# Gates and ups of three pairs of chunks by seven block products, in a fused two-layer kernel on one core

## The chip, the cores and the metric

The kernel runs on 1 core of one Trainium2 chip. The metric is the device time of one execution in microseconds; three executions are shown for the kernel before. The engines are PE (TensorE), ACT (ScalarE), DVE (VectorE), POOL (GpSimd) and SP, which here only issues transfers.

## The reference

The input x is 2 x 1024 = 2048 tokens of 512 numbers. Two layers follow each other, each ending in a layer norm:

```python
x = layernorm(x + taylor(x) + (silu(x @ gate.T) * (x @ up.T)) @ down.T)   # gate, up: 1248 x 512
# layer 2: 56 blocks of 32 rows each; a low-rank score (16) picks one row in each block
inter = x @ c1.T @ c2.T                                  # 2048 x 1792
idx = argmax of each block of 32 in inter
h = relu(w1[idx] . x);  x = layernorm(x + sum over blocks of h * w2[idx])   # w1, w2: 1792 x 512
```

`taylor` is a sum of seven terms on 128 channels, done before the part that is changed. Layer 2 is computed densely: all 1792 products with w1, masked to the picked row of each block, then the product with w2.

## The kernel before

**Tiling.** The tokens form 4 groups (g) of 512, each of 4 tiles of 128. The 1248 rows of gate and up, padded to 1280, form 10 chunks of 128; a *unit* (g,u) takes the pair u of chunks, u = 0 to 4. The 1792 rows of w1 form 14 chunks, so that a *sparse unit* n = 7g + u takes a pair, u = 0 to 6. Gated units are counted 5g + u below, so unit 10 is (2,0). All numbers are kept as two f16 parts (high and residual), and a product takes three matmuls: high x high, high x residual, residual x high.

**A gated unit** (`unit1` and `down` on PE, line 542 its second products, line 522 its first). For each chunk j of the pair: 12 matmuls of 512 columns for the gates into the bank `pa`, 12 for the ups into `pb` (`split_product`). ACT takes silu of `pa` (line 1005), DVE multiplies by `pb` (line 1576), ACT casts the high part (line 1009), POOL makes the residual (`low`, line 1123). The down products of the unit before follow, 24 matmuls into four banks `acc`. The last one of a group is in unit (g+1,0); DVE then adds the banks to the rows (`take`) and in unit (g+1,1) normalises them (`moments`, `normalise`), which gives x1.

**Tiles.** Each of the 16 tiles of x1 is scaled and split (ACT line 1019 `x1_high`, DVE line 1668 `x1_low`), transposed by SP into `xs`, multiplied by c1 (`z_product`, line 670), cut in pieces by DVE (`cut_z`), transposed again, and scored in four parts (`scores`, line 685); DVE picks the winner in each block (`pick`, lines 1699 to 1705). Tiles 0 to 10 are done in gated units, 11 to 15 in sparse units (`Z_AT`, `PICKS_AT`, `X1_AT`).

**A sparse unit** (`seven_products`, line 776) uses a Strassen-type scheme: the pair of chunks x the two halves of 512 channels x the two halves of 512 tokens is a 2 x 2 block product, done with seven block products of 6 matmuls of 256 columns in place of eight. They run over two banks; four parts have to be taken out between them: ACT copies P1 (line 1081), the pair in `pb` (line 1085) and q (line 1089), POOL adds the kept pair (`add_products`, line 1211), DVE sums `pa` (line 1834) and `pb` (line 1844) and masks each (lines 1841, 1846). PE waits for `p1_taken` and `p57_taken` within the seven, and for `pa_masked` and `pb_masked` before the next seven.

**Block sums.** The scheme needs sums of weight blocks (S) and of x blocks (T). POOL makes each in the one buffer `quad`: `raise_quad` (a weights' job 7 operations, lines 1172 to 1186; an x job 6, lines 1177 to 1194), ACT casts the high part (`sums_high`, lines 1057 to 1060), `lower_quad` stores the residual (lines 1201 to 1204). A job's raise waits until the one before is lowered. The lists `SUM_JOBS`, `JOB_IN_SWIGLU` and `JOB_IN_SPARSE` say, by hand, in which unit each stands: between the two residuals of gated units 9, 12, 14, 17, 18, 19, and in nine of the sparse units. Each engine runs its own instructions strictly in the order written.

**w2.** The array `w2_all` (w1 and w2 of layer 2, 14 chunks) is loaded during group 0, its largest value found (`w2_max`, line 1724), and all of it is split in two parts in place by ACT (line 1027) and DVE (line 1716), in turns, in units (0,4) and (1,0).

## Time and profile before

| | before |
|---|---|
| median of 3 executions | 721.61 us (721.25 to 721.93) |
| profiled execution | 722.09 us |
| its span | 720.3 us |
| granted clock, mean | 0.998 |

The profile is one execution. Busy time is per engine within the span; PE's matmuls are pipelined, so the timeline shows each run of them some 0.16 us longer than it holds up the next, while the chain shows what each adds.

### The profile page before, as it was taken

What the parts mean: (1) busy time and instruction counts of PE and PEld (TensorE: products, weight loads), DVE (VectorE), ACT (ScalarE), POOL (GpSimd) and SP (SyncE); (2) the same over time, 40 slices, a digit from 0 to 9 for tenths busy, and PEclk for the clock granted to TensorE, in tenths of its full rate; (3) what the DMA queues carried; (4) which work ended last, traced back from release to release, by engine and by line L of the source; (5) the groups of instructions that cost most, each with busy time, mean ns of one, the idle gap of its engine ahead of it and who ended that gap; (6) DMA issues with size and microseconds to landing.
All of it is one profiled execution on the core that took longest, in us unless ns stands there. A gap on an engine that the chain in (4) does not pass through costs nothing.

```text
span 720.3 us, 10333 instructions
## 1 busy us (share of the span) xinstructions
PE 706.0 (98%) x3961; PEld 382.3 (53%) x3961; DVE 527.8 (73%) x983; ACT 267.3 (37%) x450; POOL 293.3 (41%) x278
## 2 busy tenths in 40 slices
PE   7999999999999999999999999999999999999996
PEld 2444444444444444444444456666666666667763
DVE  5979897796787778677787878948885778337236
ACT  1565457444812121221222224444334333443341
POOL 0452452211111161244215666897366435742330
PEclk9999999999999999999999999999999999999999
DMA  9637309401000110110000221122222101210101
GB/s 326 257 113 223 59 3 354 111 3 56 2 15 17 22 21 2 28 27 19 6 15 19 50 49 50 32 61 16 50 72 66 47 3 59 62 45 1 59 2 58
DMA packets 40833, 44.67 MB, mean 62 GB/s; under 512 B 25296, under 2 KB 33104, under 8 KB 39888
## 3 DMA queue, kind: packets, MB, share of 16 engines
q1 hardware_dynamic: 37808, 39.29, 17.8%
q0 software_dynamic: 2112, 4.19, 3.4%
q8 instruction: 31, 0.51, 0.3%
q10 hardware_dynamic: 864, 0.53, 0.2%
q14 instruction: 18, 0.15, 0.1%
HBM read 34.33 MB, written 4.42 MB: 54 GB/s over the span
## 4 chain that ended last, share of the span: by engine, by line
PE 73%; DVE 7%; POOL 5%; issue 2%; ACT 1%; DMA 0%; POOLq 0%; DVEq 0%; ACTq 0%
PE acc L542 27%; PE pb L522 14%; PE pa L522 13%; PE pb L776 7%; PE pa L776 6%; PE acc L619 2%; PE acc L865 1%; DVE big L1703 1%; POOL work L1123 1%; PE pick_a L685 1%; PE pick_b L685 1%; POOL quad L1177 1%; DVE small L1592 1%; POOL big L1130 1%; DVE big L1701 1%
## 5 line engine op out<-in xcount | busy, mean ns | idle before, releaser
L542 PE MATMUL acc<-big,work 128*128 128x512 f16 x1038 | 235.1, 379 | 1.5 <-POOL work L1123 1.5
L1123 POOL TENSOR_TENSOR work<-work 128x512 f16<-128x512 f32 x92 | 110.4, 1212 | 274.7 <-ACT work L1009 214.7
L542 PEld LDWEIGHTS acc<-big,work 128*128 128x128 f16 x1038 | 101.4, 98 | 117.4 <-POOL work L1123 2.0
L522 PE MATMUL pa<-xs,big 128*128 128x512 f16 x480 | 111.2, 379 | 0.0
L522 PE MATMUL pb<-xs,big 128*128 128x512 f16 x480 | 110.1, 379 | 0.0
L1834 DVE TENSOR_TENSOR pa<-pa,big 128x512 f32<-128x512 f32 x28 | 19.6, 699 | 83.3 <-ACT big L1089 69.0
L522 PEld LDWEIGHTS pa<-xs,big 128*128 128x128 f16 x480 | 46.1, 98 | 54.0
L522 PEld LDWEIGHTS pb<-xs,big 128*128 128x128 f16 x480 | 46.1, 98 | 53.3
L619 PE MATMUL acc<-big 128*128 128x512 f16 x336 | 73.9, 379 | 0.3 <-DVE big L1439 0.2
L1009 ACT ACTIVATE work<-work 128x512 f16<-128x512 f32 x40 | 25.2, 630 | 111.5 <-DVE work L1576 111.5
L1130 POOL TENSOR_TENSOR big<-work,big 128x512 f16<-128x512 f32 x27 | 37.0, 1387 | 65.6 <-ACT big L947 65.3
L1104 ACT ACTIVATE work<-work 128x512 f16<-128x512 f32 x52 | 32.3, 622 | 80.1 <-DVE work L1846 57.6
L776 PE MATMUL pb<-big 128*128 128x256 f16 x432 | 56.3, 273 | 0.0
L619 PEld LDWEIGHTS acc<-big 128*128 128x128 f16 x336 | 32.7, 98 | 40.3 <-POOL big L1130 1.2
L1005 ACT ACTIVATE work<-pa,sc 128x512 f32<-128x512 f32 x40 | 27.4, 684 | 62.1 <-PE pa L522 60.0
L1576 DVE SCALAR_TENSOR_TENSOR work<-pb,sc,work 128x512 f32<-128x512 f32 x40 | 29.8, 746 | 24.6 <-PE pb L522 24.5
L776 PE MATMUL pa<-xs,big 128*128 128x256 f16 x336 | 45.7, 273 | 0.4 <-ACT big L1081 0.4
L776 PEld LDWEIGHTS pb<-big 128*128 128x128 f16 x432 | 42.3, 98 | 4.9
L1705 DVE TENSOR_REDUCE big<-big 128x14 f16<-128x448 f16 x64 | 39.7, 620 | 2.2
L1703 DVE TENSOR_TENSOR big<-big,rev_wide 128x448 f16<-128x448 f16 x64 | 38.5, 601 | 2.2
L776 PEld LDWEIGHTS pa<-xs,big 128*128 128x128 f16 x336 | 32.4, 98 | 9.8 <-ACT big L1081 1.0
L1211 POOL TENSOR_TENSOR big<-big 128x256 f32<-128x256 f32 x28 | 20.8, 744 | 39.6 <-ACT big L1085 39.6
(219 smaller groups left out, 984.5 us busy)
## 6 DMA issues: line engine op xcount, KB each, us to landing
big<-in_w_all SPq DMA_DIRECT2D x2, 3840.0 KB, 17.0
big<-in_x_t SPq DMA_DIRECT2D x16, 256.0 KB, 8.6
rows<-in_x POOLq DMA_DIRECT2D x4, 1024.0 KB, 12.7
big<-spread_rows SPq DMA_DIRECT2D x16, 256.0 KB, 6.0
big<-in_w_all SPq DMA_DIRECT2D x2, 1536.0 KB, 11.3
big<-spread_rows SPq DMA_DIRECT2D x16, 192.0 KB, 4.9
out<-rows SPq DMA_DIRECT2D x3, 1024.0 KB, 4.4
big<-in_w_all SPq DMA_DIRECT2D x1, 2048.0 KB, 14.5
```

The source lines that it names most:

```text
L522: mm = nc.tensor.matmul(dst[:, :], weights(wp)(kc * P, P), x_part16(g, xp, kc), start=(kc == 0 and wp == xp), stop=(kc == KC - 1 and wp == 1))
L542: mm = nc.tensor.matmul(acc[t][:, :], act_part(pair, j, ap, t * P, P), weights(wp)(0, H), start=(first and ap == wp), stop=(last and ap == 1))
L619: mm = nc.tensor.matmul(acc[t][:, :], term_part(m, tp, t * P, P), fuse_part(m, fp), start=(m == 0 and tp == fp), stop=(m == G and tp == 1))
L776: mm = nc.tensor.matmul(dst, weights(k, wp), moving(k, xp), start=(first and k == 0 and wp == xp), skip_group_check=True, stop=(k == KH - ...
L1005: act.activation(act32[j], pa[:, :], ACT.Silu, scale=gate_out[:, bass.ds(g, 1)]).then_inc(silu_ready, 1)
L1009: act.activation(act_part(pair, j, 0), act32[j], ACT.Copy).then_inc(act_hi, 1)
L1104: act.activation(late_part(u, j, 0) if late else act_part(GROUPS * U1 + unit, j, 0), act32[j], ACT.Relu, scale=HID_SCALE)
L1123: nc.gpsimd.tensor_tensor(act_part(pair, j, 1), act32[j], act_part(pair, j, 0), ALU.subtract).then_inc(act_lo, 1)
L1130: nc.gpsimd.tensor_tensor(term_part(m, 1), term[n % RING], term_part(m, 0), ALU.subtract).then_inc(term_lo, 1)
L1576: v.scalar_tensor_tensor(out=act32[j], in0=pb[:, :], scalar=up_out[:, bass.ds(g, 1)], in1=act32[j], op0=ALU.mult, op1=ALU.mult).then_inc(s ...
L1703: step(v.tensor_tensor(r, h, rev_wide[:, :].rearrange("p (b j) -> p b j", j=SPARSITY), ALU.mult))
L1705: last = v.tensor_reduce(winner[:, bass.ds((tile % 2) * P + k * PB, PB)], r, axis=AX.X, op=ALU.max)
```

## The change

Gates and ups of the pairs u = 0, 1, 2 are computed by seven block products too, in seven units: (1,2), (2,0), (2,1), (2,2), (3,0), (3,1), (3,2) (`FAST_UNITS`). Group 0, and the units (1,0) and (1,1), of which the latter normalises group 0, stay plain, as do all units u = 3, 4. A fast unit runs the seven products of the gates of both chunks (24 x 512 columns become 42 x 256), the down products of one chunk, the seven of the ups, and the other down products.

- **PE** waits for the kept parts as in the sparse units, for `silu_ready` before the ups, and for `swiglu_ready` before the next unit; `pb` also waits for the sums (`sums_lo`).
- **ACT** takes P1, the pair and q twice in a unit; **DVE** sums `pa` and `pb` twice; **POOL** adds the kept pair twice.
- **Jobs.** Six weights' jobs ("v", two for each pair) and six x jobs ("y", two for each of groups 1 to 3) are added. `FIRST_JOB` and `SECOND_JOB` say in which gated units jobs stand; units 8 and 9 hold two, of which the second is raised after the unit's residuals and lowered in the next unit. The nine jobs of the sparse units keep their places.
- **Space.** The new sums lie where w2's chunks 6 to 13 were. These are loaded in group 0 for their largest value alone, and loaded again after unit (3,2) (`load_again`; chunks 12 and 13 after the last gated down product). Chunks 6 and 7 are split in unit (3,3), 8 to 11 in (3,4), 12 and 13 in sparse unit 3. `w2_max` and `w2_peak` move to (1,0) to (2,1) of group 0.
- **Tiles.** Gated units now cut tiles 0 to 8, one in each of the units u = 2, 3, 4; tile 8 is picked in sparse unit 2, tiles 9 to 15 follow there. Parts 2 and 3 of a tile are picked in the unit after. The x1 rows of group 0 are normalised in one piece.

```diff
-SUM_JOBS = (("w", 0), ("w", 1), ("w", 2), ("x", 0, 0), ("x", 0, 1), ("w", 3), ("w", 4), ("w", 5), ("w", 6),
-            ("x", 1, 0), ("x", 1, 1), ("x", 2, 0), ("x", 2, 1), ("x", 3, 0), ("x", 3, 1))
-JOB_IN_SWIGLU = {9: 0, 12: 1, 14: 2, 17: 3, 18: 4, 19: 5}
-JOB_IN_SPARSE = {0: 6, 2: 7, 3: 8, 4: 9, 5: 10, 10: 11, 12: 12, 17: 13, 19: 14}
-Z_AT = {0: 11, 4: 12, 7: 13, 11: 14, 14: 15}
-PICKS_AT = {2: (11, 0), 3: (11, 2), 5: (12, 0), 6: (12, 2), 9: (13, 0), 10: (13, 2), 12: (14, 0), 13: (14, 2), 16: (15, 0), 17: (15, 2)}
-X1_AT = {2: 12, 4: 13, 6: 14, 10: 15}
+FAST = 3
+FAST_UNITS = tuple((g, u) for g in range(1, GROUPS) for u in range(FAST) if g > 1 or u > 1)
+B0 = 2 * len(FAST_UNITS)
+EARLY = 6
+TILE_AT = {(1, 2): 0, (1, 3): 1, (1, 4): 2, (2, 2): 3, (2, 3): 4, (2, 4): 5, (3, 2): 6, (3, 3): 7, (3, 4): 8}
+IN_SWIGLU = 8
+SUM_JOBS = (("v", 2, 0), ("v", 2, 1), ("y", 1, 0), ("y", 1, 1), ("v", 0, 0), ("v", 0, 1), ("y", 2, 0), ("y", 2, 1),
+            ("v", 1, 0), ("v", 1, 1), ("w", 0), ("w", 1), ("y", 3, 0), ("y", 3, 1), ("w", 2), ("x", 0, 0), ("x", 0, 1), ("w", 3),
+            ("w", 4), ("w", 5), ("x", 1, 0), ("w", 6), ("x", 1, 1), ("x", 2, 0), ("x", 2, 1), ("x", 3, 0), ("x", 3, 1))
+FIRST_JOB = {3: 0, 4: 1, 5: 2, 6: 3, 7: 4, 8: 5, 9: 7, 10: 9, 11: 10, 12: 11, 13: 12, 14: 13, 16: 14, 17: 15, 18: 16, 19: 17}
+SECOND_JOB = {8: 6, 9: 8}
+JOB_IN_SPARSE = {0: 18, 2: 19, 3: 20, 4: 21, 5: 22, 10: 23, 12: 24, 17: 25, 19: 26}
+Z_AT = {3: 9, 5: 10, 7: 11, 10: 12, 12: 13, 14: 14, 17: 15}
+LAST_PICK_AT = {3: 8, 5: 9, 7: 10, 10: 11, 12: 12, 14: 13, 17: 14, 19: 15}
+PICKS_AT = {2: 8, 4: 9, 6: 10, 9: 11, 11: 12, 13: 13, 16: 14, 18: 15}
+X1_AT = {3: 10, 5: 11, 7: 12, 10: 13, 12: 14, 14: 15}
+LATE_SPLIT = 3
...
-        W2_PIECES = ((2, 5), (5, 8), (8, 12), (0, 2), (12, C2))
-        W2_PLAN = (0, 1, 3, 4, 8, 9, 11, 13, C2)
+        W2_PIECES = ((EARLY, 10), (10, C2), (0, 4), (4, EARLY))
+        W2_AGAIN = ((EARLY, 8), (8, 12), (12, C2))
+        W2_PLAN = (0, 1, 3, 4, EARLY)
...
+            def load_again(i):
+                c0, c1 = W2_AGAIN[i]
+                dst = words(LAST_RAW_AT, (c1 - c0) * W2_SLOT) if c0 == 12 else w2_raw[:, c0 * W2_SLOT:c1 * W2_SLOT]
+                sp.dma_start(dst, w2_all[:, c0 * W2_SLOT:c1 * W2_SLOT]).then_inc(w2_again[i], 16)
...
+            for i in range(IN_SWIGLU - 1):
                 send(i)
-            sp.wait_ge(gate_ready, LAST * C1 + 7)
-            load_spread(0, 0, range(0, 2))
-            send(LAST * TPG - 2)
-            load_spread(0, 0, range(2, BPC))
-            send(LAST * TPG - 1, False)
-            sp.wait_ge(gate_ready, LAST * C1 + 9)
+            sp.wait_ge(p34_ready, B0)
+            sp.wait_ge(pb_summed, B0)
+            load_again(0)
+            load_again(1)
+            sp.wait_ge(gate_ready, plain_chunks(LAST, 3, 0) + 1)
+            load_spread(0, 0)
+            send(IN_SWIGLU - 1)
+            sp.wait_ge(gate_ready, plain_chunks(LAST, 4, 0) + 1)
             load_spread(0, 1)
-            def pass_x1(i):
-                turn_x1(i)
-                x1_arrived(i)
+            send(IN_SWIGLU)
...
+                    def pb_free():
+                        if k:
+                            pe.wait_ge(silu_ready, n + 2)
+                        else:
+                            pe.wait_ge(swiglu_ready, n)
+                            pe.wait_ge(sums_lo, SUM_JOBS.index(("y", g, 1)) + 1)
+                        pe.wait_ge(sums_lo, SUM_JOBS.index(("v", u, k)) + 1)
+                    entry = k == 0 and not fast(*unit_before(g, u))
+                    if k:
+                        pe.wait_ge(silu_ready, n + 1)
+                    elif entry:
+                        pe.wait_ge(silu_ready, n)
+                    else:
+                        pe.wait_ge(swiglu_ready, n - 1)
+                    seven_products(b, w_block, w_sum, x_block_of(g), x_sum, pb_free, entry, between)
+                half(0, z_product(tile, tile // TPG, tile % TPG, pick_a) if tile is not None else None)
+                if early is not None:
+                    scores(early, 2, pick_a)
+                    scores(early, 3, pick_b)
+                down(g, u, kind, [0])
+                half(1)
+                if tile is not None:
+                    scores(tile, 0, pick_a)
+                    scores(tile, 1, pick_b)
+                down(g, u, kind, [1])
...
+                    if j == 0 and pair - 1 in SECOND_JOB:
+                        sums_high(SECOND_JOB[pair - 1])
+                    if j == 1 and pair in FIRST_JOB:
+                        sums_high(FIRST_JOB[pair])
+                    if (g, u, j, 0) in again:
+                        w2_high(*again[g, u, j, 0])
...
+                    if (g, u, j, 1) in again:
+                        w2_high(*again[g, u, j, 1])
...
+            def fast_swiglu(g, u, tile):
+                pair, n, b = g * U1 + u, g * C1 + u * 2, fast_block(g, u, 0)
+                take_products(b)
+                act.wait_ge(act_lo, n)
+                act.wait_ge(pa_summed, b + 1)
+                act.activation(outer(work32[:, 0:2 * GT]), halves(pa[:, :]), ACT.Silu, scale=gate_out[:, g:g + 1]).then_inc(silu_ready, 1)
+                act.wait_ge(pb_summed, b + 1)
+                act.activation(work32[:, HT:3 * HT], pb[:, :], ACT.Silu, scale=gate_out[:, g:g + 1]).then_inc(silu_ready, 1)
+                if pair - 1 in SECOND_JOB:
+                    sums_high(SECOND_JOB[pair - 1])
+                if tile:
+                    x1_high(tile)
+                take_products(b + 1)
+                if pair in FIRST_JOB:
+                    sums_high(FIRST_JOB[pair])
+                act.wait_ge(swiglu_ready, n + 2)
+                for j in range(2):
+                    act.activation(act_part(pair, j, 0), act32[j], ACT.Copy).then_inc(act_hi, 1)
+                if tile == 0:
+                    x1_high(tile)
...
+            for n in range(1, GROUPS * U1):
+                g, u = n // U1, n % U1
+                if fast(g, u):
+                    add_products(fast_block(g, u, 0))
+                if n - 1 in SECOND_JOB:
+                    lower_quad(SECOND_JOB[n - 1])
+                if fast(g, u):
+                    if n in FIRST_JOB:
+                        raise_quad(FIRST_JOB[n])
+                    add_products(fast_block(g, u, 1))
+                    if n in FIRST_JOB:
+                        lower_quad(FIRST_JOB[n])
+                    low(n, 0, n * 2)
+                    low(n, 1, n * 2 + 1)
+                    continue
+                low(n, 0, n * 2)
+                if n in FIRST_JOB:
+                    raise_quad(FIRST_JOB[n])
+                    lower_quad(FIRST_JOB[n])
+                low(n, 1, n * 2 + 1)
+                if n in SECOND_JOB:
+                    raise_quad(SECOND_JOB[n])
...
+            def sum_pa(b):
+                dve.wait_ge(p57_added, b + 1)
+                dve.wait_ge(q_taken, b + 1)
+                v.tensor_tensor(pa[:, :], pa[:, :], p1_and_57_of[0], ALU.add).then_inc(pa_summed, 1)
+            def sum_pb(b):
+                dve.wait_ge(p34_ready, b + 1)
+                v.tensor_tensor(halves(pb[:, :]), halves(pb[:, :]), q_kept_of[0].unsqueeze(1).broadcast_to([P, 2, HT]), ALU.add).then_inc(pb_summed, 1)
+            def fast_swiglu(g, u):
+                n, b = g * C1 + u * 2, fast_block(g, u, 1)
+                gated = outer(work32[:, 0:2 * GT])
+                sum_pa(b)
+                dve.wait_ge(silu_ready, n + 1)
+                dve.wait_ge(pa_summed, b + 1)
+                v.scalar_tensor_tensor(out=gated, in0=halves(pa[:, :]), scalar=up_out[:, g:g + 1], in1=gated,
+                                       op0=ALU.mult, op1=ALU.mult).then_inc(swiglu_ready, 1)
+                sum_pb(b)
+                dve.wait_ge(silu_ready, n + 2)
+                dve.wait_ge(pb_summed, b + 1)
+                v.scalar_tensor_tensor(out=work32[:, HT:3 * HT], in0=pb[:, :], scalar=up_out[:, g:g + 1], in1=work32[:, HT:3 * HT],
+                                       op0=ALU.mult, op1=ALU.mult).then_inc(swiglu_ready, 1)
...
+            def fast_unit(g, u, early, tile):
+                b = fast_block(g, u, 0)
+                sum_pa(b)
+                sum_pb(b)
+                if early is not None:
+                    pick(early, 2, pick_a)
+                    pick(early, 3, pick_b)
+                if tile is not None:
+                    cut_z(tile, pick_a)
+                    x1_low(tile + 1)
+                if u == 1:
+                    moments(g - 1, 1)
+                    normalise(g - 1, x1_ready, middle=lambda: fast_swiglu(g, u))
+                    if g == 1:
+                        x1_low(0)
+                else:
+                    fast_swiglu(g, u)
+                if tile is not None:
+                    first_picks(tile)
+                if u == 0:
+                    take(g - 1, down_ready, down_out[:, g - 1:g])
+            def plain_unit(g, u, early, tile):
+                if early is not None:
+                    pick(early, 2, pick_a)
+                swiglu(g, u, 0)
+                if early is not None:
+                    pick(early, 3, pick_b)
+                if (g, u) == (GROUPS - 1, 4):
+                    w2_low(8, 10)
+                if tile is not None:
+                    cut_z(tile, pick_a)
+                    x1_low(tile + 1)
+                if u == 1:
+                    moments(g - 1, 1)
+                    normalise(g - 1, x1_ready, middle=lambda: swiglu(g, u, 1))
+                    x1_low(0)
+                    return
                 swiglu(g, u, 1)
-                if nxt is not None:
-                    pick(tile, 3, pick_b)
-            def first_unit1(g, last=None, halves=False):
-                if halves:
-                    swiglu(g, 1, 0)
-                    moments(g - 1, 1, (0, 1))
-                    normalise(g - 1, x1_ready, (0, 1), low=g * TPG - TPG)
-                    swiglu(g, 1, 1)
-                    moments(g - 1, 1, (2, 3))
-                    normalise(g - 1, x1_ready, (2, 3))
-                    return
-                moments(g - 1, 1)
-                swiglu(g, 1, 0)
-                normalise(g - 1, x1_ready, low=g * TPG - TPG)
-                swiglu(g, 1, 1)
-                if last is not None:
-                    pick(last, 3, pick_b)
-            def tile_units1(g):
-                for u in range(2, U1):
-                    unit1(g, u, (g - 1) * TPG + (u - 2), (g - 1) * TPG + (u - 1))
-            dve.wait_ge(w2_lo, 2 * C2 + 4)
+                if (g, u) == (GROUPS - 1, 3):
+                    w2_low(EARLY, 8)
+                if (g, u) == (GROUPS - 1, 4):
+                    w2_low(10, 12)
+                if tile is not None and tile < IN_SWIGLU:
+                    first_picks(tile)
...
+                if n == LATE_SPLIT:
+                    w2_low(12, C2)
+                if n in PICKS_AT:
+                    first_picks(PICKS_AT[n])
+                    pick(PICKS_AT[n], 2, pick_a)
```

`seven_products` is the former code with its waits handed in; the sparse units use it as before.

## Rows read from the trace of the kernel before

**Rows 1.** The page, busy time of each engine.
```profile
PE 706.0 (98%) x3961; PEld 382.3 (53%) x3961; DVE 527.8 (73%) x983; ACT 267.3 (37%) x450; POOL 293.3 (41%) x278
```

**Rows 2.** Stretches: us, busy us (instructions) of each engine, PEclk, DMA share, GB/s.
```profile
208.00:290.00 82.00, 82.00 (x412) 37.76 (x411) 63.74 (x138) 17.61 (x28) 19.88 (x19) 1.00 0.08 17
...
455.00:530.00 75.00, 73.54 (x504) 47.87 (x503) 56.95 (x106) 30.99 (x60) 50.36 (x50) 1.00 0.23 49
```

**Rows 3.** What PE waited for: us, times, longest.
```profile
PE acc L542 <- POOL work L1123: 1.5, 2, 0.8
PE pick_a L685 <- DMA big<-big: 1.4, 1, 1.4
```

**Rows 4.** The chain of waits in unit (1,0): start, us, what.
```profile
187.46 2.59 PE pa L522 x12
```

**Rows 5.** The chain in sparse unit 8, and its second products.
```profile
509.51 0.66 PE pa L776 x6
510.17 1.31 PE pb L776 x12
...
514.10 5.18 PE acc L542 x24
```

**Rows 6.** Groups of instructions on ACT and DVE, shapes apart: busy us, mean ns.
```profile
L1834 DVE TENSOR_TENSOR pa<-pa,big 128x512 f32<-128x512 f32 x28 | 19.6, 699 | 83.3 <-ACT big L1089 69.0 <-POOL big L1211 14.3
...
L1576 DVE SCALAR_TENSOR_TENSOR work<-pb,sc,work 128x512 f32<-128x512 f32 x40 | 29.8, 746 | 24.6 <-PE pb L522 24.5
L1005 ACT ACTIVATE work<-pa,sc 128x512 f32<-128x512 f32 x40 | 27.4, 684 | 62.1 <-PE pa L522 60.0 <-DVE big L1716 2.0
...
L1085 ACT ACTIVATE big<-pb 128x512 f32<-128x512 f32 x28 | 16.7, 597 | 22.8 <-PE pb L776 22.8
...
L1081 ACT ACTIVATE big<-pa 128x256 f32<-128x256 f32 x28 | 10.6, 380 | 33.8 <-PE pa L776 33.8
```

**Rows 7.** POOL in order of time, kept pair and a raise, 430:437.
```profile
430.79 0.72 POOL L1211 TENSOR_TENSOR big<-big 128x256 f32<-128x256 f32 x1 [0.72 <-ACT big L1085]
431.47 1.15 POOL L1172 TENSOR_TENSOR quad<-big 128x512 f32<-128x512 f16 x1
...
436.38 0.73 POOL L1186 TENSOR_TENSOR quad<-quad 128x256 f32<-128x256 f32 x1
```

**Rows 8.** ACT in order of time, four casts of w2 at 174.
```profile
173.79 2.55 ACT L1027 ACTIVATE big<-big,sc 128x512 f16<-128x512 f32 x4
```

**Rows 9.** POOL, a job of weights, 254:264.
```profile
254.39 1.60 POOL L1172 TENSOR_TENSOR quad<-big 128x512 f32<-128x512 f16 x1
...
259.92 0.73 POOL L1186 TENSOR_TENSOR quad<-quad 128x256 f32<-128x256 f32 x1
...
262.53 1.64 POOL L1202 TENSOR_TENSOR first_sums<-quad,first_sums 128x768 f16<-128x768 f32 x1
```

**Rows 10.** POOL, a job of x sums, 384:394.
```profile
384.46 2.71 POOL L1177 TENSOR_TENSOR quad<-xs 128x512 f32<-128x512 f16 x2
...
391.61 2.13 POOL L1204 TENSOR_TENSOR big<-quad,big 128x1024 f16<-128x1024 f32 x1 [1.17 <-ACT big L1060]
```

**Rows 11.** PE in order of time, the starts of units (1,3) and (1,4).
```profile
229.70 2.11 PE L522 MATMUL pa<-xs,big 128*128 128x512 f16 x9
...
246.20 2.11 PE L522 MATMUL pa<-xs,big 128*128 128x512 f16 x9
```

**Rows 12.** POOL, the first residual of unit (1,3).
```profile
236.77 1.16 POOL L1123 TENSOR_TENSOR work<-work 128x512 f16<-128x512 f32 x1 [5.43 <-ACT work L1009]
```

**Rows 13.** DVE in order of time, a pick and the start of the next.
```profile
257.44 0.61 DVE L1699 TENSOR_REDUCE big<-pick_b 128x14 f32<-128x448 f32 x1
258.09 0.62 DVE L1701 TENSOR_TENSOR big<-pick_b,big 128x448 f16<-128x448 f32 x1
...
259.82 0.62 DVE L1699 TENSOR_REDUCE big<-pick_a 128x14 f32<-128x448 f32 x1
```

**Rows 14.** The stretch after the last product of PE, columns as in rows 2.
```profile
713.66:720.30 6.64, 0.00 (x1) 0.00 (x0) 3.72 (x16) 0.70 (x1) 0.00 (x0) 0.79 0.21 79
```

More of the change, by code:

```diff
@@ new lines, in unit @@
+            def unit(g, u):
+                early, tile = TILE_AT.get(unit_before(g, u)), TILE_AT.get((g, u))
+                kind = "last" if u == 0 else "first" if u == 1 else "middle"
+                if fast(g, u):
+                    fast_unit(g, u, kind, early, tile)
+                    return
+                unit1(g, u, early, tile)
+                down(g, u, kind, [0])
+                if tile is not None and tile < IN_SWIGLU:
+                    scores(tile, 0, pick_a)
+                    scores(tile, 1, pick_b)
+                down(g, u, kind, [1])
@@ L751, in _, with second2 @@
             down(1, 0, "last")
-            for g in range(1, GROUPS - 1):
-                group1(g)
-                unit1(g + 1, 0, g * TPG - 1, (g - 1, TPG - 1))
-                down(g + 1, 0, "last", scored=g * TPG - 1)
-            group1(GROUPS - 1)
-            def second2(g, u, kind, after_first):
+            for n in range(U1 + 1, GROUPS * U1):
+                unit(n // U1, n % U1)
+            def second2(g, u, kind, after):
                 before = g * U2 + u - 1
@@ L768, in second2, with hidden_products @@
                                    halved=(g == GROUPS - 1 and kind != "last"))
[L769 to L780 removed]
+                    after(j)
+            def hidden_products(g, u):
                 n = g * U2 + u
[L783 removed]
                 def w_block(c, half):
```

434 lines of the change are left out of this document (245 added, 189 removed).

## The prediction

> **What bounds the kernel now.** I read the page first (the busy shares), then the stretches, then the waits of PE, then the chain piece by piece. PE is busy 706.0 us of a 720.3 us span [rows 1]. In the stretches it is busy all 82 us of 208:290 and misses 1.46 us of 455:530, while DVE is at 57 to 64 us and POOL at 20 to 50 us of these, all at a granted clock of 1.00 [rows 2]. Its waits in both phases are a scores product that waited 1.4 us for a transposed tile and second products that waited 1.5 us for POOL [rows 3]. So every product taken from PE counts in full, and every product that another engine hands over late is new time. Nothing else is to be asked.
>
> **The saving.** A plain unit's chain holds four runs of 12 products of 512 columns at 2.59 us [rows 4] and 5.18 us of down products, as long as the second products [rows 5]. The sparse phase already works by seven block products: 0.66 + 1.31 + 1.31 + 1.31 = 4.59 us for the 42 products of 256 columns [rows 5]. Gates (or ups) of a pair cost 2 x 2.59 = 5.18 us now and 4.59 us by blocks, so 0.59 us less each; 7 units x 2 = 14 of them give **-8.3 us**. Per product that is 216 ns against 109 ns: the cost goes by columns, and seven eighths of the columns are left.
>
> The Trainium skill (TensorE: Matmul & The Clock Gate, section Back-to-back issue gap) gives a sustained roofline of about 131 ns for a product of 512 columns, and 81 ns for one of 128; by that rule 24 wide products would take 3.1 us, 42 of half the width at least 3.4 us, and the change would lose 0.3 us a block. The trace disagrees: 216 ns each [rows 4].
>
> **Tiles and scores.** The products of all 16 tiles stay, in other places: 0. The 1.4 us wait for a transposed tile stood in unit (3,2), where DVE's multiplication sat behind a block-sum job; the unit is now a fast one and has its tile cut earlier: -1.4. The two POOL waits follow from sparse jobs that keep their units: 0.
>
> **The second loading of w2's last 8 chunks** (4 MB more) lies on DMA engines that are 8 to 23% busy [rows 2]. It is issued at the end of unit (3,2) and wanted 18 us later: 0, with up to 2 us if a transpose waits behind it.
>
> **A fast unit by itself.** Prices: ACT takes P1 and q in 0.38, pb in 0.60, silu 0.69; DVE adds in 0.70 and multiplies in 0.75 [rows 6]; POOL adds the kept pair in 0.72 [rows 7]; a cast is 0.64, a quarter of [rows 8]. From the unit's start: q is taken at 3.7, pa summed at 4.4, silu at 5.1, pb's silu at 6.0; the ups start at 7.2. Their pa is gated at 12.4 and their pb at 13.9; the next unit wants them at 14.3 and 15.0. DVE's 2.8 us more per unit and ACT's takes are thus hidden, with 0.5 to 2 us of slack; about 0.8 us in all for units where it is short (the first, and u = 1 with the moments): **+0.8**.
>
> **POOL's jobs.** A job holds one buffer, so jobs run one behind the other, and each needs ACT's cast between raise and lower. A weights' job took 254.39 to 264.13 = 9.74 us, of it 6.26 for the raise [rows 9]; an x job 384.46 to 393.74 = 9.28 [rows 10]; with DVE quiet the raise took 5.6 [rows 7]. Before, six jobs stood in the gated units, one in a unit. Now twelve more come before them, one in nearly every unit from (0,3) on, and units 8 and 9 have two each. Following POOL from the first residual of unit 8, which starts 7.1 us into a unit (229.70 to 236.77 [rows 11, 12]):
> - residual 1.12, job 5 9.74, residual 1.2, job 6 9.28, residual 1.15, job 7 9.28: it ends at 7.1 + 31.8 = 38.9.
> - PE comes to unit 10's pb, which needs job 7 (the second x sum of group 2), at 2 x 16.50 (229.70 to 246.20 [rows 11]) + 1.31 = 34.3. **Wait one: 4.6.**
> - From there (0): PE needs 1.31 + 0.66 + 1.31, scores 0.38, down 2.59 = 6.25 to the ups. POOL has the residual 1.15, then the raise of job 8 (queued ahead of the kept products) 5.6, the add 0.72; DVE 0.70, silu 0.69: 8.9. **Wait two: 2.65.**
> - From the ups' start: second silu until 0.7, ACT's cast of job 8 until 1.95, lower 4.2, raise of job 9 10.2, add 10.9, sum and gate 12.4. PE is through at 7.2, plus 0.35 for a late P1: **wait three 4.85**; then 0.8 for pb and 0.3 for the next P1.
>
> Sum 4.6 + 2.65 + 0.35 + 4.85 + 1.1 = **+13.6**. By raises alone on their port the three waits are 1.6 us less; all of them beside DVE, 1.3 more. Job 13 ends as unit 15 wants it. A unit with one job and no backlog fits: its raise ends at 9.7, when the second kept pair is ready.
>
> **The end of the gated phase.** Late w2 conversions now sit on ACT and DVE in (3,3) and (3,4), four casts 2.55 us [rows 8] at each place. From the start of (3,3): silu, then ACT waits for the job raised 8.9 to 14.9, casts it until 16.0, splits chunks 6 and 7 until 18.6, DVE until 19.4, and only then picks tile 7 (a pick beside POOL is 2.38, its comparison done after 1.27 [rows 13]). PE wants that comparison at 19.25 and gets it at 20.65: 1.4. DVE's three picks end at 26.6, its multiplication at 27.4, against 26.4: 1.0. ACT then does copy, tile, 4 casts, silu, the job (raised until 35.5), copy, 4 casts until 39.9 and takes P1 at 40.3; PE has been waiting since 37.8: 2.5. **+4.9.**
>
> **Sparse phase.** Two more tiles, so three picks in one unit (about 7.4) and cut, pick, x1 in the next. Beside 2.9 us of masks DVE's load per unit is at most 10.5 against 9.8 to 10.3 of PE, and comes back in the next; masks can be 2.5 late before ACT's take is: 0, up to 2.5.
>
> **Sum.** The profiled run took 722.09 us, 1.8 around its 720.3 span. 722.1 - 8.3 - 1.4 + 0.8 + 13.6 + 4.9 = 731.7; the median is 0.5 less than that run: **731 us**, 1.3% slower.
>
> **Rivals.**
> 1. *The jobs keep up (faster).* It needs POOL's chain from unit 8 to be 4.6 us shorter, or ACT's order to hold nothing up. For it: before, fifteen such jobs cost PE 1.5 us in all [rows 3]. Against: there they stood singly, and 9.28 is the shortest full job beside swiglus. Then 722.1 - 9.7 + 0.8 and 0 to 3 for the boundary, less 0.5: 713 to 716. It decides at the x sums of unit 10: lowered before PE's 34.3, faster. 0.15.
> 2. *Only the boundary costs*: 717 to 719. 0.05. *Only the jobs cost*, the boundary absorbed: 725 to 728. 0.08.
> 3. *The clock falls too.* After PE's last product at 713.66 the granted clock averaged 0.79 over 6.64 us against 1.00 before [rows 14], so idle time did bring it to 1.2 GHz (0.21 x 6.64 = 1.4 us lost, which is 2.8 us at half rate). Waits of 4.6 and 4.85 could do it. No row shows the rise; a block run at half rate costs 4.6 more, and after waits one and two the slack of the next wait takes it. With masks late as well: 736 to 742. 0.08.
> 4. The forecast: 727 to 736. 0.64.
>
> The Trainium skill (same page, section What's actually happening) says that idle time takes TensorE from 2.4 to 1.2 GHz; the trace's end agrees.
>
> **How the numbers follow.** About 0.2% (1.4 us) can be told from no change. Faster: rival 1 and the first of 2 = 0.20. The jobs alone, the forecast and rival 3 are slower: 0.78, which leaves 0.02 for the same. The range leaves out rival 1 and the top of rival 3: 718 to 739. The forecast's own range is 727 to 736.
>
> **What would show it.** Right: fourteen runs of 4.59 in place of 5.18; PE idle some 13 us between the start of unit (2,0) and that of (2,1), released by POOL's low sums, then by ACT's silu behind POOL's add, then by DVE's gated pa; 4 to 5 us around the last two gated units, released by DVE's compare, DVE's multiplication and ACT's take of P1; no idle in (2,3) to (3,2) over 1 us; the sparse units at 9.8 to 10.3. Wrong: raises of 4 us, sums ready before unit 10, or PE idle in the sparse phase beyond 3 us.

## The result, and the profile after

| | before | after |
|---|---|---|
| median, us | 721.8 (721.25 to 722.48, 5 runs) | 752.04 (751.45 to 753.72, 5 runs) |
| profiled execution, us | 722.09 | 751.9 |
| its span, us | 720.3 | 750.1 |
| PE busy, us | 706.0 | 710.4 |
| mean granted clock of TensorE | 0.998 | 0.987 |

The ratio is 1.0424 (1.0410 to 1.0439): 4.2% slower, 30.2 us. Forecast were 731 us and a range of 718 to 739; the sign was right, the size was not.

The page of the kernel after, busy time of each engine, answers to [rows 1]:

```profile
PE 710.4 (95%) x4213; PEld 409.2 (55%) x4213; DVE 573.1 (76%) x1000; ACT 295.4 (39%) x510; POOL 401.4 (54%) x388
```

PE has 8.3 us of columns less and is busy 4.4 us longer. So the products themselves became slower, beside 32.7 us of idle time (7.4 before), counted as PE's waits of 0.15 us and more. The stretches, columns as in [rows 2]:

```profile
180.00:213.00 33.00, 32.51 (x151) 14.44 (x149) 20.36 (x34) 8.79 (x14) 23.41 (x23) 1.00 0.00 1
213.00:246.00 33.00, 27.48 (x175) 16.18 (x174) 20.37 (x33) 11.23 (x21) 15.19 (x16) 0.95 0.09 18
246.00:290.00 44.00, 38.48 (x217) 21.02 (x216) 31.54 (x52) 12.07 (x22) 35.78 (x38) 0.96 0.08 16
290.00:345.00 55.00, 48.63 (x318) 29.97 (x316) 38.25 (x74) 17.89 (x34) 40.28 (x45) 0.97 0.04 9
345.00:400.00 55.00, 54.31 (x369) 34.59 (x368) 45.36 (x83) 18.97 (x35) 31.12 (x31) 1.00 0.06 13
400.00:450.00 50.00, 46.12 (x253) 23.72 (x251) 39.98 (x64) 17.58 (x30) 28.69 (x28) 0.97 0.39 115
```

The reader is to see that PE falls short in two places, 213 to 345 and 400 on, that the clock is below 1.00 in just these, and that 345 to 400, with its fast units, is sound: a fast unit that waits for nothing takes 14.35 us (379.34 to 393.69). Now PE in order of time at its six longest waits, at the next longest (1.63 us) and at the short wait two (start, us, what; in brackets the idle time before, and what ended it), with the products behind some of them:

```profile
224.12 0.34 PE L737 MATMUL pick_a<-c_parts,xs 128*128 128x32 f16 x8 [3.96 <-SPq L506]
...
225.72 4.34 PE L609 MATMUL acc<-big,work 128*128 128x512 f16 x12
...
269.96 0.36 PE L752 MATMUL pick_a<-c_stack,big 128*128 128x448 bf16 x1 [1.63 <-DMA big<-big]
...
276.90 2.72 PE L796 MATMUL pb<-big 128*128 128x256 f16 x12 [2.49 <-issue]
...
285.74 0.83 PE L796 MATMUL pa<-xs,big 128*128 128x256 f16 x6 [0.88 <-ACT work L1181]
286.41 1.47 PE L796 MATMUL pb<-big 128*128 128x256 f16 x12
...
290.34 2.75 PE L609 MATMUL acc<-big,work 128*128 128x512 f16 x12
297.75 1.46 PE L796 MATMUL pa<-xs,big 128*128 128x256 f16 x6 [4.66 <-DVE work L1995]
...
426.24 0.36 PE L752 MATMUL pick_a<-c_stack,big 128*128 128x448 bf16 x1 [3.69 <-DMA big<-big]
...
452.48 0.83 PE L796 MATMUL pa<-big,first_sums 128*128 128x256 f16 x6 [2.67 <-ACT big L1163]
...
504.32 0.36 PE L752 MATMUL pick_a<-c_stack,big 128*128 128x448 bf16 x1 [2.92 <-DVE big L1909]
```

276.90, 285.74 and 297.75 are the prediction's waits one, two and three; 452.48 is the predicted end of the gated phase. 224.12 (the z product waits for x1's tile 0 to be turned), 426.24 (in unit (3,3), for the turned z of tile 7) and 504.32 (at the end of sparse unit 4, for a compare of DVE) were not foreseen, nor were 218.03 (1.57 us for the second y sum), 269.96 (1.63) and 344.13 (1.15, like it for a turned tile). Behind a wait the same products take longer: twelve of 512 columns 4.34 us at 225.72 and 2.75 at 290.34, twelve of 256 columns 2.72 at 276.90 and 1.47 at 286.41.

### The profile page after: what moved, and what is told of

It reads as the page before. It is cut to its first block, busy times and chain, and to the rows that moved or that the text cites. A ratio compares the mean times of both kernels' runs of the same rounds, so it can differ in the third digit from the quotient of the medians.

```text
span 750.1 us, 11148 instructions
## 1 busy us (share of the span) xinstructions
PE 710.4 (95%) x4213; PEld 409.2 (55%) x4213; DVE 573.1 (76%) x1000; ACT 295.4 (39%) x510; POOL 401.4 (54%) x388
## 4 chain that ended last, share of the span: by engine, by line
PE 41%; DVE 22%; POOL 12%; issue 9%; ACT 3%; DMA 1%; SPq 0%; DVEq 0%; POOLq 0%; ACTq 0%
PE acc L609 16%; PE pb L796 10%; PE pa L796 8%; PE acc L686 2%; POOL work L1292 2%; DVE big L1924 2%; DVE sc L1933 2%; PE pb L589 2%; DVE big L1504 2%; DVE big L1911 2%; PE pa L589 1%; DVE big L1909 1%; POOL quad L1360 1%; POOL quad L1357 1%; DVE small L1800 1%
## 5 line engine op out<-in xcount | busy, mean ns | idle before, releaser
L796 PE MATMUL pb<-big 128*128 128x256 f16 x684 | 91.5, 279 | 4.6 <-issue 4.1
L796 PEld LDWEIGHTS pb<-big 128*128 128x128 f16 x684 | 67.9, 100 | 15.0 <-issue 4.6
L796 PE MATMUL pa<-xs,big 128*128 128x256 f16 x504 | 69.4, 276 | 6.0 <-DVE work L1995 4.7
L589 PE MATMUL pa<-xs,big 128*128 128x512 f16 x312 | 72.2, 379 | 0.4 <-ACT work L1137 0.4
L589 PE MATMUL pb<-xs,big 128*128 128x512 f16 x312 | 71.6, 379 | 0.1
L1273 ACT ACTIVATE work<-work 128x512 f16<-128x512 f32 x52 | 32.3, 622 | 90.7 <-DVE work L2082 62.3
L796 PEld LDWEIGHTS pa<-xs,big 128*128 128x128 f16 x504 | 49.3, 99 | 20.6 <-DVE work L1995 5.4
L1403 POOL TENSOR_TENSOR big<-big 128x256 f32<-128x256 f32 x42 | 31.7, 754 | 51.8 <-ACT big L1167 51.7
L686 PEld LDWEIGHTS acc<-big 128*128 128x128 f16 x336 | 32.7, 98 | 40.3 <-POOL big L1299 1.2
L589 PEld LDWEIGHTS pb<-xs,big 128*128 128x128 f16 x312 | 30.0, 98 | 35.4 <-DVE work L1784 0.6
L1924 DVE SCALAR_TENSOR_TENSOR big<-big,sc 128x512 f16<-128x512 f32 x28 | 32.7, 1225 | 10.8 <-ACT big L1211 10.8
L1167 ACT ACTIVATE big<-pb 128x512 f32<-128x512 f32 x42 | 25.1, 597 | 38.9 <-PE pb L796 38.7
```

The source lines that it names most:

```text
L589: mm = nc.tensor.matmul(dst[:, :], weights(wp)(kc * P, P), x_part16(g, xp, kc), start=(kc == 0 and wp == xp), stop=(kc == KC - 1 and wp == 1))
L686: mm = nc.tensor.matmul(acc[t][:, :], term_part(m, tp, t * P, P), fuse_part(m, fp), start=(m == 0 and tp == fp), stop=(m == G and tp == 1))
L796: mm = nc.tensor.matmul(dst, weights(k, wp), moving(k, xp), start=(first and k == 0 and wp == xp), skip_group_check=True, stop=(k == KH - ...
L1167: act.activation(p57_kept_of[late], pb[:, :], ACT.Copy).then_inc(p57_taken, 1)
L1273: act.activation(late_part(u, j, 0) if late else act_part(GROUPS * U1 + unit, j, 0), act32[j], ACT.Relu, scale=HID_SCALE)
L1403: nc.gpsimd.tensor_tensor(p1_and_57_of[late][:, HT:GT], kept[:, 0:HT], kept[:, HT:GT], ALU.add).then_inc(p57_added, 1)
```

## The experiments

All are timed against the kernel before on the same chip. "Over before" is the difference of the two medians there, since the kernel before had 721.5 to 722.2 us from one chip to the next; the kernel after is 30.2 us over before.

**e2, e3, e4: when the jobs run, and what delays x1's tile.**

```diff
 e2: y(2) jobs behind v(1,0); two jobs stand in (0,2)/(0,3) and (1,0), no longer in (1,3) and (1,4)
-FIRST_JOB = {3: 0, 4: 1, 5: 2, 6: 3, 7: 4, 8: 5, 9: 7, 10: 9, ...
-SECOND_JOB = {8: 6, 9: 8}
+FIRST_JOB = {3: 1, 4: 2, 5: 3, 6: 5, 7: 6, 8: 7, 9: 8, 10: 9, ...
+SECOND_JOB = {2: 0, 5: 4}
 e3: unit (1,1)
-normalise(g - 1, x1_ready, middle=lambda: swiglu(g, u, 1))
-x1_low(0)
+normalise(g - 1, x1_ready, middle=lambda: (x1_low(0), swiglu(g, u, 1)))
 e4: both
```

> The same jobs in other places: units 8 and 9 hold one each, the first job starts at the end of unit 2 and unit 5 holds two. Theory A (POOL's chain of jobs through units 8 and 9 is what PE waits for in units 10 and 11) expects the waits there (2.5, 0.9, 4.7 us, and a slow clock after) to go: 740 to 744, with up to 3 us given back around unit 6 and 7. The rival, that a fast unit's own chain over ACT and DVE is too long, expects them to stay: 750 or more.

> In unit (1,1) DVE splits tile 0 of x1 right after the second row is normalised, before the multiplication, in place of after the fourth row. If PE's 4.0 us wait in unit 7 is for that tile, it goes, and with it the slow clock after it: 745 to 748. If the tile is only the last of several that are late there (POOL's low sums, the kept pair), at most 1 us is won: 751 or more.

> Both edits together. If the two waits are separate costs, the gains add: 734 to 740. If they feed on each other (an earlier unit 7 only makes POOL later in unit 10), it is within 2 us of the better of the two alone.

Measured: e2 740.4 us (1.0245 to 1.0280 times before), e3 747.6 (1.0325 to 1.0381), e4 738.4 (1.0214 to 1.0245). e2 gains 11.6 us: all three waits are gone, so they were the backlog of units 8 and 9. A new one stands in (1,2):

```profile
222.75 1.46 PE L796 MATMUL pa<-big 128*128 128x256 f16 x6 [4.24 <-ACT big L1163]
```

ACT takes P1 there; ahead of it on ACT is a cast behind POOL's raise in (1,1). In e3, 4.4 us faster than the kernel after, the 3.96 us are gone. Wait two is 2.23 there and not 0.88, but this is not e3's doing: in e7 below, which is the kernel after up to the sparse phase, it is 2.22. What differs is the products behind wait one, at full speed in e3 and e7 and slow in the kernel after (276.90, 2.72 us). PE in e7:

```profile
275.07 1.47 PE L796 MATMUL pb<-big 128*128 128x256 f16 x12 [2.48 <-issue]
...
283.90 0.83 PE L796 MATMUL pa<-xs,big 128*128 128x256 f16 x6 [2.22 <-ACT work L1181]
```

So the 1.25 us that the slow products cost were taken back by the next wait, whose end ACT's silu sets, behind POOL's add. In e4 the wait for P1 is 3.69, and 13.6 us are gained where 11.6 and 4.4 would make 16.0; the executions of e3 lie 5 us apart, so this shortfall is not clear of the noise. The time fits both expectations (734 to 740, and 2.0 us below e2).

**e6: that wait.** As e4, but no job in (1,1), two in (0,3) and (1,0) instead; the diff is against e4.

```diff
-FIRST_JOB = {3: 1, 4: 2, 5: 3, 6: 5, 7: 6, ...       SECOND_JOB = {2: 0, 5: 4}
+FIRST_JOB = {3: 1, 4: 3, 5: 4, 7: 6, ...             SECOND_JOB = {2: 0, 3: 2, 5: 5}
```

> Both moves of e4 and one more: unit (1,1) raises no block sums at all (the job of its first place goes to units (0,3) to (1,0), where two stand in one unit once more), so that ACT has no cast of sums between (1,1)'s second silu and the P1 of (1,2). Theory: the wait of 3.69 us for P1 in unit (1,2) comes from ACT's cast behind POOL's raise in (1,1) and goes, with the fall of the clock behind it: 733 to 736 us. Rival (P1 is late because DVE normalises in (1,1) and gates late): the wait stays over 2 us, 737 to 739.

Measured 741.6 us (1.0267 to 1.0302), slower than e4. The 3.69 us became 0.63, but waits of 1.44, 3.98 and 1.33 stand at 185, 192 and 197 us (e4 has 1.02 at 176 and 1.06 at 190). There ACT's casts for the second job of (0,3) and the job of (0,4), at 180.60 and 192.77, stand ahead of its casts of w2, and DVE's splits of w2, 8.46 us in one run, ahead of its multiplication. Neither side of the expectation held: the cause was right, the cure moved the wait ahead, into (1,0). Ten jobs in front of unit (2,1) do not fit anywhere without a wait.

**e10: the jobs' work taken away.** The v and y jobs, twelve of them (the expectations of e5 and e10 say ten, which is the number ahead of unit (2,1)), are left at 16 columns on POOL and ACT, and PE multiplies other blocks of the same shape. What is left out is the computing of the sums.

```diff
+if kind in "vy":
+    nc.gpsimd.tensor_tensor(quad[:, 0:16], pairs[0][0][:, 0:16], pairs[0][1][:, 0:16], ALU.add)...
+    return
```

> The kernel after with the ten jobs for gates and ups (v and y) cut to 16 columns in each of their operations on POOL and ACT; PE multiplies other blocks of the same shape in place of the sums, so that it does as many products. What is left out is the computing of these sums. Theory (jobs on POOL make all the waits between 210 and 320 us and, by their use of the port, DVE's slow normalising): waits one, two and three, 1.57 at sums_lo, 3.96 for x1 tile 0 and the clock's falls there all go; left are the saving of 8.3 and the edge of e5: 721.5 + 10 - 8.3 + 1 = 723 to 726 us. Rival (a fast unit costs by itself, in takes and adds, much of what it saves): 729 to 733.

Measured 725.5 us (1.0033 to 1.0067), 3.8 over before: 26.4 us less than the kernel after, and within the theory's range. Its stretch of [rows 2] is PE 81.47 of 82 at a clock of 1.00 (after: 70.96 at 0.96), POOL 25.13 instead of 55.60:

```profile
208.00:290.00 82.00, 81.47 (x524) 49.15 (x523) 58.33 (x118) 24.93 (x51) 25.13 (x37) 1.00 0.10 16
```

The spans differ by 25.1 us: 18.2 of idle time (32.7 against 14.5) and 6.8 of the same 4213 products taking longer (busy 710.4 against 703.6). Most of that second part is the clock: by the mean clocks of the two executions, 0.987 and 0.994, the kernel after lost 9.8 us of full speed and e10 4.4, 5.4 apart (an estimate from the rounded means). The 26.4 us hold all that the jobs do: POOL's backlog, ACT's casts behind it, DVE slowed beside POOL, and the clock; these were not taken apart further. The x1 tile is explained too. DVE in unit (1,1) of the kernel after, then POOL in it, then DVE in e10:

```profile
213.00 1.00 DVE L1838 TENSOR_SCALAR rows<-rows,small 128x512 f32<-128x512 f32 x2
...
215.93 3.58 DVE L1838 TENSOR_SCALAR rows<-rows,small 128x512 f32<-128x512 f32 x2
219.43 0.68 DVE L1876 SCALAR_TENSOR_TENSOR big<-rows,big 128x512 f16<-128x512 f32 x1
```

```profile
215.81 2.12 POOL L1392 TENSOR_TENSOR big<-quad,big 128x1024 f16<-128x1024 f32 x1 [2.86 <-ACT big L1226]
217.89 1.34 POOL L1292 TENSOR_TENSOR work<-work 128x512 f16<-128x512 f32 x1
```

```profile
211.30 0.99 DVE L1839 TENSOR_SCALAR rows<-rows,small 128x512 f32<-128x512 f32 x2
212.21 0.68 DVE L1877 SCALAR_TENSOR_TENSOR big<-rows,big 128x512 f16<-128x512 f32 x1
```

The second pair of rows takes 3.58 us and ends at 219.51, 0.28 behind the second of POOL's two instructions (219.23); in e10, where POOL is idle for most of it, the same pair takes 0.99.

**e5: the fast units taken away,** all else as after.

```diff
-FAST_UNITS = tuple((g, u) for g in range(1, GROUPS) for u in range(FAST) if g > 1 or u > 1)
+FAST_UNITS = ()
 the twelve v and y jobs dropped, the others in the units of the kernel after; plain units take the rows at u = 0
```

> All gated units plain: no seven block products for gates and ups, none of the ten jobs for them, the six jobs of before at their old units; the changed places of tiles, casts and of w2's second loading stay as in the kernel after. Theory (the two halves of the change cost separately): the excess of the last gated units and of sparse units 0, 4 and 5, some 11 to 14 us of the kernel after, stays, and everything between 210 and 400 us goes: 730 to 736 us, with PE's waits at the scores of unit (3,3) by DMA, at the first P1 of the sparse phase and at sparse unit 4's compare still there. Rival (the late waits come from PE's, DVE's and POOL's lateness in the fast units): 721 to 726 us.

Measured 731.5 us (1.0126 to 1.0158), 10.1 over before. PE in order of time:

```profile
407.93 0.55 PE L750 MATMUL pick_a<-c_stack,big 128*128 128x448 bf16 x1 [4.66 <-DMA big<-big]
432.85 0.83 PE L794 MATMUL pa<-big,first_sums 128*128 128x256 f16 x6 [1.51 <-ACT big L1161]
484.48 0.36 PE L750 MATMUL pick_a<-c_stack,big 128*128 128x448 bf16 x1 [2.91 <-DVE big L1907]
```

The first product behind the first wait takes 0.55 us, that behind the third 0.36: the clock again. The three waits are there in e10 too, with 3.90, 2.45 and 2.92 us (sum 9.3, here 9.1). So the change is two costs that hardly touch: 10.1 us at the end of the gated phase, whatever the units, and 20.1 us by the fast units with their jobs. The latter are -6.3 by the units (3.8 of e10 less 10.1) and +26.4 by the jobs. e5's jobs stand as in the kernel after (11, 12 and 16 to 19), not at the units of before, as its expectation says.

**e7, e8, e9: moving one thing at the end of the gated phase.**

```diff
 e7:  -X1_AT = {3: 10, 5: 11, ...          +X1_AT = {4: 10, 5: 11, ...
 e8:  load_again(0); load_spread(0, 0); send(7), with load_again(1) now behind its turn_z(7)
 e9:  e5, e8's load, chunks 10 and 11 split in sparse unit 0,   -LATE_SPLIT = 3   +LATE_SPLIT = 2
```

> The kernel after with x1's tile 10 lowered (ACT's and DVE's parts) in sparse unit 4, not in unit 3. Theory: the compare for which sparse unit 4 waits 2.92 us is late because w2's last split (4.57 us) and this lowering (2.65 us beside POOL) stand ahead of it on DVE; 2.65 us less there takes 2.5 us of the wait and part of the clock's fall: 747 to 750 us. Rival (DVE only passes it on; unit 4's own masks behind POOL's add are late): same time as after within 1 us, the wait moving to the next unit.

> The kernel after with the second part of w2's second loading (2 MB) issued behind the transposing of tile 7's z, not ahead of it. Theory (traffic: the transposing DMA waits behind the 3 MB and the spread rows): landing falls from 4.3 to about 2.5 us, the wait of 3.69 us in unit (3,3) shrinks to 1.5 to 2.2: 749 to 751 us. Rival (DVE cuts z late, the DMA is as ever): wait and time as in the kernel after within 0.5 us.

> e5 (all gated units plain) with the splitting of w2's second loading placed otherwise: chunks 10 and 11 in sparse unit 0 and not in (3,4), chunks 12 and 13 in sparse unit 2 and not in 3, the 2 MB loading behind the transposing of tile 7's z. Theory (the 10 us of e5 over the kernel before are three places where split, picks and masks stand in one unit, and units beside them have room): the wait for P1 (1.51) and that at sparse unit 4 (2.91) go, the 4.66 us for tile 7's scores halves: 724 to 727 us. Rival (the load of DVE and ACT over these nine units is too much altogether, as e7 and e8 hint, where a wait taken away came back at the next step): 729 to 732.

Measured: e7 753.5 us (1.0424 to 1.0464), e8 751.95 (1.0409 to 1.0443), e9 736.1 (1.0184 to 1.0214), 14.4 over before where e5 is 10.1. In e7 sparse unit 4's 2.92 us fell to 0.41, and unit 5's z product waited 4.06 for the tile. In e8 the DMA's 3.69 fell to 1.15, and a wait of 2.73 for a compare came 8.5 us behind it. In e9 the wait of e5 at 432.85 shrank to 0.41, that at 484.48 went, and one of 8.67 us stood in sparse unit 2. DVE in e9:

```profile
406.09 4.92 DVE L1925 SCALAR_TENSOR_TENSOR big<-big,sc 128x512 f16<-128x512 f32 x4 [3.33 <-ACT big L1210]
410.94 0.61 DVE L1908 TENSOR_REDUCE big<-pick_a 128x14 f32<-128x448 f32 x1
...
460.25 4.53 DVE L1925 SCALAR_TENSOR_TENSOR big<-big,sc 128x512 f16<-128x512 f32 x4
464.70 0.61 DVE L1908 TENSOR_REDUCE big<-pick_a 128x14 f32<-128x448 f32 x1
```

At 460.25 the moved split stands ahead of unit 2's picks, and PE waits for these. From 433 to 472 us, over sparse units 1 and 2, DVE idles 0.22 us, so there is no gap to take it. But ahead of 406.09 DVE idles 3.33 us for ACT's casts, with tile 7's picks queued behind: there it is order, not load.

**e12, e14, e15: taking that end apart.**

```diff
 e12: e5, ACT's and DVE's splits of chunks 6 to 13 cut to 16 columns, chunks 0 to 5 read in their place
 e14: e12 and e8's load
 e15: e5, e8's load, and on ACT:
-again = {(3, 3, 1, 0): (EARLY, 8), (3, 4, 0, 1): (8, 10), (3, 4, 1, 1): (10, 12)}
+again = {(3, 3, 1, 0): (EARLY, 8), (3, 4, 0, 1): (8, 10), (3, 4, 1, 0): (10, 12)}
+if (g, u, j, 0) in again:
+    w2_high(*again[g, u, j, 0])
 if j == 1 and pair in FIRST_JOB:
     sums_high(FIRST_JOB[pair])
-if (g, u, j, 0) in again: ...
```

> e5 (all gated units plain) with the splitting of w2's eight chunks loaded again cut to 16 columns in each of its 32 operations on ACT and DVE; PE and POOL read chunks 0 to 5 in their place, so that they do as much as before. What is left out is the splitting of these chunks. The loading itself stays. Theory (the 10 us at the end of the gated phase are the splitting, some 19 us of DVE and 10 us of ACT put into nine units that had no room): waits of 4.66, 1.51 and 2.91 us go or shrink below 1.2 each: 722 to 725 us. Rival (the tiles' new places do it: three picks in one unit, and tile 7's late cut): over 728, the waits still there.

> e12 (all gated units plain, the splitting of the second loading cut to 16 columns) with the 2 MB loading issued behind the transposing of tile 7's z. Theory (the 4.34 us are the transposing DMA behind 3 MB of loads): the wait falls to about 1.1 and nothing takes its place, as DVE has room: e12's time less 3.2 and less the clock's fall behind the wait: 722.5 to 725 us. Rival (the wait is that of DVE's cut or of the queue's order): 727 to 729.

> e5 (all gated units plain, all the splitting done) with the 2 MB loading behind the transposing of tile 7's z, and on ACT the casts of chunks 6 and 7 in (3,3) and of 10 and 11 in (3,4) ahead of the casts of the block-sum job of that unit, for which POOL is still raising; nothing else is moved. Theory (ACT's order makes the compare and P1 late: DVE idles 3.33 us for these casts in e9): the 4.66 us become 1.1, no wait for the compare over 1 us, none for P1; sparse unit 4's 2.91 stays: 725 to 728 us. Rival (the amount of work): waits move on to the next step, 729 to 732.

Measured: e12 728.1 us (1.0067 to 1.0097), 5.9 over before; e14 723.55 (1.0016 to 1.0034), 1.8; e15 727.9 (1.0068 to 1.0095), 6.1. e12 is at the edge between its two expectations: without the split's length the waits at the first P1 and at sparse unit 4 are gone, and the one for tile 7 stays, 4.34 us. e14 takes it to 0.91 by the place of one load, worth 4.1 us with the clock behind it. Taken away in this order, e5's 10.1 us are 4.2 of splitting, 4.1 of the load's place and 1.8 of neither. e15 keeps all the work and gets 4.0 back by the order of one load and two casts; in e8 the load's place alone gave nothing. PE in e15:

```profile
405.51 0.36 PE L751 MATMUL pick_a<-c_stack,big 128*128 128x448 bf16 x1 [1.09 <-DMA big<-big]
456.07 0.36 PE L751 MATMUL pick_a<-c_stack,big 128*128 128x448 bf16 x1 [1.11 <-DVE big L1908]
480.43 0.55 PE L751 MATMUL pick_a<-c_stack,big 128*128 128x448 bf16 x1 [2.92 <-DVE big L1908]
```

In (3,3) and (3,4) the wait for the compare (2.73 in e8, 1.72 in e9) and that for P1 (1.51 in e5, 2.86 in e8) are gone, so ACT's order had made both. The 1.11 stands in sparse unit 2.

**e11, e13, e16: fewer fast units.** Only (2,0), (2,1), (3,0), (3,1). Four of the twelve jobs go, and six in place of ten stand ahead of (2,1): y(2), v(0) and v(1), two of each.

```diff
-FAST = 3
+FAST = 2
-FIRST_JOB = {3: 0, 4: 1, 5: 2, 6: 3, 7: 4, 8: 5, 9: 7, 10: 9, ...   SECOND_JOB = {8: 6, 9: 8}
+FIRST_JOB = {5: 0, 6: 1, 7: 2, 8: 3, 9: 4, 10: 5, ...               SECOND_JOB = {}      (e11, with e9's end)
+FIRST_JOB = {4: 0, 5: 1, 7: 2, 8: 3, 9: 4, 10: 5, ...               SECOND_JOB = {}      (e13; e16 with e15's end)
```

> Block products in units (2,0), (2,1), (3,0) and (3,1) alone (eight of the fourteen pairs of gates or ups), their six jobs ahead of (2,1) one in a unit from (1,0) on, and the placing of e9 at the end of the gated phase. Theory (a job per unit fits, two don't): no wait over 1.2 us between 180 and 400 us, the gated phase 8 x 0.59 = 4.7 us shorter than in e9, so e9's time less 3.5 to 4.7: 720 to 723 if e9 is at 725, 725 to 728 if it is at 730. Rival (a late sum at (2,0) or normalising beside POOL in (1,1) still costs 3 us or more): e9's time less 1.5, or more than it.

> Block products in units (2,0), (2,1), (3,0) and (3,1) alone, as in e11, but with the end of the gated phase as in the kernel after, and the y jobs in (0,4) and (1,0), so that no job stands beside the normalising of (1,1). Theory (e11's wait of 1.83 us for x1's tile came from that job; the gain of 4.7 us then reaches the end): no wait over 1.2 us from 180 to 390 us, e5's time less 4.0 to 4.7: 727 to 728 us. Rival (DVE and ACT at the end of the gated phase are what is waited for, so that PE's earlier arrival is turned into longer waits there): 729.5 to 732.

> e13 (block products in (2,0), (2,1), (3,0), (3,1) alone) with the loading and ACT's order of e15. Theory (the gain of 8 x 0.59 us reaches the end when nothing waits there): e15's time less 4.0 to 4.7, so 721 to 724 us, which would be the time of the kernel before within 0.3%. Rival (given back at sparse unit 4 or at tile 7): e15's time less 0 to 2.

Measured: e11 735.4 us (1.0177 to 1.0208), e13 732.0 (728.8 to 732.8; 1.0124 to 1.0158), e16 725.7 (1.0028 to 1.0056). e11 gains 0.75 on e9, by its rival: a job beside the normalising of (1,1) makes the tile late by 1.83 us, and 2.74 us are lost at a compare where e9 loses 1.72. e13 has the gated phase clean up to (3,3) and is 9.8 over before, where e5 is 10.1: the rival's side. Its profiled run (728.8, mean clock 0.993) is 2.8 us faster than e5's median; in the other three (731.3 to 732.8) the clock was 0.989 to 0.991. e16 gains 2.2 on e15 of the 4.7 taken out, between its two expectations: the wait in sparse unit 2 is 1.79 and not 1.11, and behind the same wait at unit 4 (2.93 and 2.92) the clock was 0.57 over 7 us and not 0.77, some 1.4 us (an estimate, 7 us x 0.20). Of the changed kernels that leave nothing out it is the best, and 0.4% slower than the kernel before. No version found here beats that.

## Why the prediction was right and wrong

- **The saving and a fast unit by itself** (-8.3 + 0.8 = -7.5): -6.3 measured, and a unit without waits takes 14.35 us. Right within 1.2. Twelve narrow products again start 1.31 us apart (286.41 to 287.72), 109 ns each. The sustained roofline that the Trainium skill gives (TensorE: Matmul & The Clock Gate, Back-to-back issue gap) is not borne out here either.
- **POOL's jobs** (+13.6, the step that failed most): they cost 26.4. The chain itself was followed well: from unit 8's first residual to the last lowering 245.64 to 276.80 = 31.2 us, forecast 31.8; wait three 4.66, forecast 4.85. Wait one was 2.49 instead of 4.6: the chain was 0.6 shorter, and PE came 1.6 later, having waited 1.63 at 269.96 in unit (1,4). Wait two was 0.88 instead of 2.65, since the slow products ahead of it took 1.25 of it (2.22 in e7). What was missing stands in unit (1,2), 1.57 us for a y sum and 3.96 us for x1's tile, and in the waits of 1.63 and 1.15 for turned tiles. The failed step is where the followed chain began: at unit 8, with the jobs of units 3 to 7 taken as free ("A unit with one job and no backlog fits"), and DVE's operations beside them, the normalising of (1,1) above all, priced as if POOL were idle.
- **The clock** (rival 3, chance 0.08, 736 to 742 with late masks): it came. Of e10's gain 6.8 us are the same products taking less time, most of it the clock. After the waits of 3.96 and 4.66 us the granted clock was 0.95 and 0.97 in the stretches. A wait followed by a fall made the products behind it 1.4 to 3.0 us longer (an estimate, 7 us x (1 - 0.80) to 7 us x (1 - 0.57)), which should have been in the likeliest case once two waits over 4.5 us were forecast. The prediction's reason against it, that the slack of the next wait takes the loss, held behind wait one; behind the waits of 3.96, 4.66 and 2.92 us nothing shows it. The Trainium skill (TensorE: Matmul & The Clock Gate, What's actually happening) says that idle time takes TensorE from 2.4 to 1.2 GHz; the granted clocks agree.
- **The end of the gated phase** (+4.9, less 1.4 = 3.5; measured 10.1). The wait for P1 was right (2.67, forecast 2.5). The second loading, put at 0 (up to 2 us if a transpose waits) since the DMA engines were 8 to 23% busy in two other stretches, failed: behind 3 MB of loads and the spread rows, PE waits 3.69 us for tile 7's turned z (4.34 in e12), and moving one 2 MB load gives 4.1 us back where DVE has room (e12 to e14). In 400:450, where the loading falls, the share was 0.39 in the kernel after. The -1.4 rests on a wait put into the wrong unit. In the kernel before it stood in (3,3), not in (3,2): the unit begins at 392.76, and one more gated unit, from 410.80, lies ahead of the sparse phase at 427.30. That unit stayed plain, and its wait grew from 1.37 to 3.69:

```profile
392.76 2.11 PE L522 MATMUL pa<-xs,big 128*128 128x512 f16 x9
...
402.26 0.36 PE L685 MATMUL pick_a<-c_stack,big 128*128 128x448 bf16 x1 [1.37 <-DMA big<-big]
...
410.80 2.10 PE L522 MATMUL pa<-xs,big 128*128 128x512 f16 x9
...
427.30 1.47 PE L776 MATMUL pa<-xs,big 128*128 128x256 f16 x12
```

- **Sparse phase** (0, up to 2.5): 2.92 us at unit 4, and the clock behind it (0.76). That DVE's load "comes back in the next" unit overlooked that the split of the last two chunks, a cut, a pick and x1's tile fall into unit 3, and that DVE, from 463.83 in unit 1 to 504.32, idles 0.33 us. The bound of 2.5 was nearly right; the value taken was not. DVE in unit 3 of the kernel after:

```profile
488.54 4.57 DVE L1924 SCALAR_TENSOR_TENSOR big<-big,sc 128x512 f16<-128x512 f32 x4
...
497.55 2.65 DVE L1876 SCALAR_TENSOR_TENSOR big<-rows,big 128x512 f16<-128x512 f32 x1
```

- **The range** (to 739) missed since it took one rival at a time. The misses all have one sign: 12.8 us at the jobs (26.4 less 13.6), 6.6 at the end of the gated phase with unit 4 (10.1 less 3.5) and 1.2 at the saving make 20.6 of the 21 us between 731 and 752. The sign was not luck: both costs that the forecast names came, and larger.

What stays open: 1.8 us between e14 and the kernel before; how the 26.4 us divide among backlog, DVE beside POOL and clock; and how much of e13's scatter is the clock.

## What to carry to other kernels

Where an engine at 98% is relieved by moving work to a helper, follow the helper's queue from its first new job, not from where it first looks full, and price other engines' work beside it from rows where both are busy. A forecast wait on TensorE belongs into the sum twice, as idle time and as slow products behind it: here always from 3.5 us on, and 12 times in 27 from 2.2 to 3.1. The second part is given back only where another engine sets the end of the next wait (wait two). A mean DMA share of other stretches says nothing of a small transfer that PE waits for: ask what large load is issued in front of it, since another place for that load may cost nothing (e14).
